# Graph network on one core: a longer buffer ring for the first edge pass, and the lookup's block differences made by TensorE and ScalarE

## The chip, the cores and the metric

One Trainium2 chip, one of its cores. The metric is the device time of one execution in microseconds (us), lower is better. The kernel before took 4364.09 us, the median of three runs (4363.95 to 4365.29).

## What is computed

A graph of 6250 nodes (padded to 6656, that is 52 blocks of 128) and 100000 edges sorted by destination (padded to 784 tiles of 128) goes through four layers. Each one normalizes x, takes the ReLU, runs a message pass over the edges and adds its result to x. Only the first layer, a graph attention, is touched:

```python
h = relu(layernorm(x))
hw = h @ W
a_s = hw @ att_src
a_d = hw @ att_dst
e = leaky_relu(a_s[src] + a_d[dst], 0.2)
m = segment_max(e, dst)
p = exp(e - m[dst])
out = segment_sum(hw[src] * (p / segment_sum(p, dst)[dst]), dst)
x = x + out + bias
```

In the kernel the sums over edges run on rows of h (128 floats of a node), and the product with W comes after them.

## The kernel before, in words

A tile is 128 edges, one per partition; a chunk is C = 8 tiles. For each tile GpSimd issues one indirect DMA that fetches the 128 source rows of h from `table[0]` in DRAM into a slot of a row buffer (a buffer holds one chunk, 4 KB per partition). These gathers are issued one after another by GpSimd, 784 for the layer. The ring has `RING0` = 16 buffers, four that live all through the kernel (`m.rows`) and twelve in `m.more`. `gather_straight` (L873) issues those gathers that need no free buffer, that is the first 16 * 8 = 128, spread over the phases ahead of the edge pass. A phase is a block: all engines begin it together and meet at its end. In order:

- `norm_phase` (L239) writes h to `table[0]` and its transpose to `m.hT` (a 128 x 6656 tile, 26 KB per partition).
- `setup_phase` (L107): SyncE loads five 392 KB index arrays, VectorE (after all five, `loaded` 80) splits the source index into its low 7 bits (`lo`, stored to DRAM) and its block number (`src_hi`, kept), and works out windows. GpSimd issues 14 gathers (`IN_SETUP`).
- `attention_tables_phase` (L407): TensorE spreads a_d over the nodes from `m.hT`; a_s is brought into columns. GpSimd issues 30 gathers (`IN_TABLES`).
- `lookup_phase` (L485) finds a_s[src] for every edge in 49 steps of 16 tiles. In a step SyncE loads the low bits broadcast to all partitions (`place`, 512 KB, ring of 4); VectorE turns them into a one-hot (`make`, L535, into `onehot`, bf16); TensorE multiplies it by a_s in three bf16 parts, 48 products of 52 columns (L560), which gives a candidate for each of the 52 blocks; GpSimd makes `away`, the block number counted from 0 to 51 less the edge's own (L521); VectorE keeps the candidate where `away` is zero (`pick`, L541) and sums over the blocks (`keep`, L547). VectorE's order is make of the next step, pick, keep. GpSimd's order is one `away`, one gather.
- `segment_max_phase` (L563): scans on VectorE and three trips through DRAM. GpSimd issues 20 gathers (`IN_MAXIMA`).
- `attention_edges` (L1102): GpSimd issues the last 15 of the first 128 gathers, then walks the ring (`gather_long_ring`, L954, which issues through L839): a gather waits until VectorE has freed its buffer (`rows_free`). For each of 98 chunks VectorE makes weights (`weigh`), TensorE clears a bank (L789) and adds up 8 tiles by a product with the rows (L1217) and one with ones (L1218), and VectorE adds the window into `acc` (L1193) and frees the buffer. VectorE's loop body holds 8 chunks, TensorE's as many as the ring.
- `attention_output` (L2086): SyncE sends three lines of sums to DRAM and brings them back in another layout, loads weights, then x in four slabs of 768 KB (or 832 KB). TensorE multiplies `acc` and `m.hT` by W, GpSimd adds the bias to x, ScalarE scales, and VectorE works out the shares of the softmax (L2167 to L2182) and adds both parts to x.

The later layers are not touched. What sets the order around the change is the program order of each engine's queue; there is no planner. Durations below belong to these lines.

Of the kernel before, what the change touches and what calls it, by code (L numbers as in the profile page):

```python
# [10 lines left out]
RING0 = 16  # L11
# [4 lines left out]
IN_SETUP, IN_TABLES, IN_MAXIMA = 14, 30, 20  # L16
# [90 lines left out]
def setup_phase(nc, k, m, early):  # L107

    T, NP, N = k.T, k.NP, k.N
    with ExitStack() as ctx:  # L110
# [7 lines left out]
        hi_i = sb("su_hi", [P, T], I32)  # L118
        span = sb("su_span", [P, 2, T], F32)
# [3 lines left out]
        lo_ready = sem("su_lo_ready")  # L123
        chain = sem("su_chain")
        stored = sem("su_stored")
        with nc.Block() as block:
            @block.sync
            def _(sp):
# [4 lines left out]
                sp.dma_start(hi_i[:], k.dram["src_el"]).then_inc(loaded, 16)  # L133
# [3 lines left out]
                sp.wait_ge(stored, 16)  # L137
                sp.wait_ge(loaded, 80)
# [7 lines left out]
            def _(v):  # L146
                ch = Chain(v, chain)
                v.wait_ge(loaded, 80)

                ch.step(v.tensor_scalar(lo_i[:], lo_i[:], P - 1, None, ALU.bitwise_and))  # L150
                v.tensor_copy(lo_b[:], lo_i[:]).then_inc(lo_ready, 1)
                ch.step(v.tensor_scalar(hi_i[:], hi_i[:], 7, None, ALU.logical_shift_right))
                ch.add(v.tensor_copy(m.src_hi[:], hi_i[:]))
# [331 lines left out]
def lookup_phase(nc, k, m, s_el, early):  # L485
# [5 lines left out]
    with ExitStack() as ctx:  # L491
# [4 lines left out]
        away, masked = [sb(f"away{b}", [P, L, NB], F32) for b in range(2)], [sb(f"masked{b}", [P, L, NB], F32) for b in range(2)]  # L496
        block_ps = [ctx.enter_context(nc.psum_tensor(f"lu_ps{b}", [P, L, PER], F32)) for b in range(2)]
        place_ready, place_free = [sem(f"place_ready{r}") for r in range(4)], sem("place_free")
        onehot_ready, block_ready, away_ready = sem("onehot_ready"), sem("block_ready"), sem("away_ready")
# [3 lines left out]
        steps = T // L  # L503
        with nc.Block() as block:
# [11 lines left out]
            def _(pool):  # L516
                pool.sem_inc(masked_ready, 2)

                for n in range(steps):
                    pool.wait_ge(masked_ready, n + 1)  # L520
                    pool.tensor_tensor(away[n % 2][:], m.iota_f[:, 0:NB].unsqueeze(1).to_broadcast([P, L, NB]),  # L521
                                       m.src_hi[:, n * L:(n + 1) * L].unsqueeze(2).to_broadcast([P, L, NB]),
                                       ALU.subtract).then_inc(away_ready, 1)
                    gather_straight(pool, k, m, early, k.table[0], IN_SETUP + IN_TABLES + n, 1)

            @block.vector
            def _(v):
                v.sem_inc(place_free, 4)
                v.sem_inc(block_ready, 2)
                v.sem_inc(picked, 2)  # L530

# [5 lines left out]
                def pick(at):  # L537
                    v.wait_ge(block_ready, at.n + 3)
                    v.wait_ge(away_ready, at.n + 1)
                    v.wait_ge(picked, at.n + 1)  # L540
                    v.scalar_tensor_tensor(masked[at.b][:], away[at.b][:], 0.0, block_ps[at.b][:, :, 0:NB], ALU.is_equal, ALU.mult).then_inc(masked_ready, 1)  # L541
# [11 lines left out]
            def _(pe):  # L553

                def product(at):
                    pe.wait_ge(onehot_ready, at.n + 1)
# [5 lines left out]
                    ins.then_inc(block_ready, 1)  # L562
                skewed(pe, steps, Item, [(0, product)])  # L563


def segment_max_phase(nc, k, m, s_el, early):
# [4 lines left out]
    with ExitStack() as ctx:  # L571
# [18 lines left out]
        with nc.Block() as block:  # L590
# [16 lines left out]
            def _(pool):  # L607
                gather_straight(pool, k, m, early, k.table[0], IN_SETUP + IN_TABLES + T // (2 * C), IN_MAXIMA)
# [254 lines left out]
def early_rows(nc, name, rows, begun):  # L863
# [4 lines left out]
    early.gathered = [[nc.alloc_semaphore(f"{name}gathered{r}_{q}") for q in range(2)] for r in range(len(rows))]  # L868
    early.idx_loaded, early.dst_loaded = nc.alloc_semaphore(name + "idx_loaded"), nc.alloc_semaphore(name + "dst_loaded")
    early.all = sum(early.gathered, []) + [early.idx_loaded, early.dst_loaded]  # L870
# [1976 lines left out]
```

## Time and profile before

| | before |
|---|---|
| median of three runs | 4364.09 us |
| the profiled execution's own time | 4362.5 us |
| its span, first to last instruction | 4360.7 us |
| TensorE, VectorE, ScalarE, GpSimd busy | 84%, 49%, 31%, 66% |
| TensorE clock, mean of the span | 0.667 of 2.4 GHz |
| setup block begins | 41.6 us |
| lookup block begins, ends | 105.6 us, about 269.7 us |
| first bank of the edge pass cleared, last sum added | 306.7 us, 1158.0 us |
| attention output, first transfer issued | 1161.3 us |

Times are measured from the first instruction. Matmul, weight load, VectorE, ScalarE and GpSimd instructions have a start and a duration; "idle before" is the time that an engine stood still ahead of an instruction, with what ended it. An indirect DMA on GpSimd counts as busy while GpSimd writes its descriptors; the rows themselves land later. In a table by stretches the column PEclk is the TensorE clock that was granted, as a share of 2.4 GHz (0.50 is 1.2 GHz).

### The profile page before, as it was taken

Reading aid. Unit: us, or ns where it says so; the run is one execution under the profiler, and the core shown is the slowest. Engines: PE = TensorE matmul, PEld = TensorE weight load, DVE = VectorE, ACT = ScalarE, POOL = GpSimd, SP = SyncE. Lnnn points to the kernel's source line nnn. Section 1 sums busy time; section 2 is a strip of 40 time slices with the busy share of each in tenths; the row PEclk is TensorE's granted clock in tenths of the full one; section 3 lists DMA queues with packets and bytes.
Section 4 is the critical chain, followed back from the end, with each engine's and each line's share of the span. In section 5 each row is a group of like instructions: output and inputs, shape, how many; then the busy total and the mean of one; then the engine's idle time right before and its main releaser. Section 6 shows DMA issues by size and latency. Waiting matters only on the chain. (4 is left out here: it accounts for less than half of the span.)

```text
span 4360.7 us, 76651 instructions
## 1 busy us (share of the span) xinstructions
PE 3646.0 (84%) x20596; PEld 3028.2 (69%) x20597; DVE 2136.9 (49%) x6551; ACT 1362.1 (31%) x1910; POOL 2881.8 (66%) x2980
## 2 busy tenths in 40 slices
PE   3649999777668999999996958888888865999997
PEld 1649999766637888888886846656555643777775
DVE  4874444333455555555554844444444446444442
ACT  2000000000041111111112847666666655444441
POOL 4877777777526777777751047777777764777772
PEclk7555555555575555555556978777777775999998
DMA  4532222222263333333322043333333333111112
GB/s 121 197 116 54 53 53 53 53 53 53 63 208 106 79 80 79 79 78 78 79 68 84 21 127 113 100 104 104 104 99 105 104 82 85 50 50 51 50 51 52
DMA packets 258518, 364.29 MB, mean 84 GB/s; under 512 B 53070, under 2 KB 179461, under 8 KB 258309
## 3 DMA queue, kind: packets, MB, share of 16 engines
q0 software_dynamic: 90624, 185.78, 16.5%
q1 hardware_dynamic: 167689, 176.37, 13.4%
q14 instruction: 148, 1.21, 0.1%
q8 instruction: 57, 0.93, 0.1%
HBM read 319.53 MB, written 42.41 MB: 83 GB/s over the span
## 5 line engine op out<-in xcount | busy, mean ns | idle before, releaser
L839 POOL DMA_INDIRECT m_rows<-table,e_idx x832 | 794.2, 955 | 255.8 <-issue 228.6
L839 POOL DMA_INDIRECT m_more<-table,e_idx x480 | 453.7, 945 | 145.6 <-issue 118.5
L1218 PE MATMUL e_agg<-e_weights,m_ones 128*128 128x32 f32 x1568 | 481.8, 401 | 0.0
L839 POOL DMA_INDIRECT m_hT<-table,e_idx x416 | 394.1, 947 | 125.7 <-issue 107.6
L1218 PEld LDWEIGHTS e_agg<-e_weights,m_ones 128*128 128x128 f32 x1568 | 428.5, 333 | 0.0
L839 POOL DMA_INDIRECT e_rows<-table,e_idx x352 | 342.0, 971 | 105.7 <-issue 103.9
L1217 PE MATMUL e_agg<-e_weights,m_more 128*128 128x16 f32 x1152 | 339.8, 375 | 78.3 <-issue 66.3
L1653 PE MATMUL e_z<-e_edge,e_w 128*128 128x512 f32 x392 | 262.8, 806 | 167.2 <-DVEq L1734 152.2
L805 POOL DMA_INDIRECT m_rows<-table,e_idx x320 | 307.9, 962 | 116.0 <-issue 82.3
L1217 PEld LDWEIGHTS e_agg<-e_weights,m_more 128*128 128x128 f32 x1152 | 311.5, 330 | 104.2 <-issue 104.2
L1542 PE MATMUL e_out<-e_counts,e_nodes 128*128 128x256 bf16 x2964 | 383.6, 280 | 0.0
L1882 PE MATMUL e_x<-e_key,e_rows_T 128*128 x1568 | 373.9, 420 | 2.5 <-DMA e_key<-key_dram 2.5
L1384 ACT ACTIVATE e_counts<-e_count 128x832 bf16<-128x832 f32 x304 | 262.4, 864 | 321.8 <-PE e_count L1535 321.2
L1882 PEld LDWEIGHTS e_x<-e_key,e_rows_T 128*128 128x128 f32 x1568 | 352.4, 330 | 9.3 <-issue 7.1
L1542 PEld LDWEIGHTS e_out<-e_counts,e_nodes 128*128 128x128 bf16 x2964 | 297.6, 100 | 79.5 <-issue 5.5
L1664 PEld LDWEIGHTS e_z<-e_w,e_filt 128*128 128x128 f32 x1568 | 257.4, 257 | 50.3 <-issue 50.3
L1664 PE MATMUL e_z<-e_w,e_filt 128*128 128x128 f32 x1568 | 282.4, 354 | 0.0
L1143 ACT ACTIVATE e_pl<-e_diff 128x8 f32<-128x8 f32 x98 | 20.6, 210 | 801.6 <-DVE e_diff L1177 801.6
L1653 PEld LDWEIGHTS e_z<-e_edge,e_w 128*128 128x128 f32 x392 | 88.0, 250 | 256.4 <-DVEq L1734 158.2
L1675 PE MATMUL e_agg<-e_onehot,e_message 128*128 128x16 f32 x1568 | 228.1, 289 | 12.5 <-DVE e_message L1746 12.3
L1843 ACT ACTIVATE e_p<-e_p 128x32 f32<-128x32 f32 x98 | 22.5, 229 | 684.8 <-DVEq L2011 684.8
L1675 PEld LDWEIGHTS e_agg<-e_onehot,e_message 128*128 128x128 f32 x1568 | 218.3, 223 | 20.6 <-issue 13.1
(315 smaller groups left out, 7057.3 us busy)
## 6 DMA issues: line engine op xcount, KB each, us to landing
e_edge<-edge_T SPq DMA_DIRECT2D x98, 512.0 KB
lu_place<-lo_dram SPq DMA_DIRECT2D x49, 512.0 KB, 3.8
e_key<-key_dram SPq DMA_DIRECT2D x98, 256.0 KB
m_rows<-table,e_idx POOLq DMA_INDIRECT x1152, 2.5
key_dram<-key_out SPq DMA_DIRECT2D x13, 1024.0 KB, 4.7
table<-m_rows SPq DMA_DIRECT2D x39, 256.0 KB, 2.6
e_rows<-table,e_idx POOLq DMA_INDIRECT x528, 2.6
m_more<-table,e_idx POOLq DMA_INDIRECT x480, 2.5
```

Source lines behind the costliest of these rows:

```text
L805: pool.indirect_dma_start(rows[:, t, :], None, table, bass.IndirectOffsetOnAxis(ap=idx[:, t:t + 1], axis=0)).then_inc(landed[q], 16)
L839: pool.indirect_dma_start(rows[:, t, :], None, table, bass.IndirectOffsetOnAxis(ap=idx[:, t:t + 1], axis=0)).then_inc(landed[t * len(lande ...
L1143: act.activation(pl[b][:, :, 0], diff[:], ACT.Exp).then_inc(p_ready, 1)
L1217: pe.matmul(to[:, 0, cols], s.rows[at.r][:, t, :], both[:, t, 0, :], start=False, stop=False)
L1218: ins = pe.matmul(to[:, 1:3, cols], m.ones[:], both[:, t, :, :], start=False, stop=(t == C - 1))
L1384: act.activation(counts[at.b][:, :, t * W_NARROW:(t + 1) * W_NARROW].rearrange("p (h n) w -> p h n w", h=2), count_ps[t % 2][:, :, 0:PART] ...
L1542: ins = pe.matmul(out_ps[b][:, 0:L * W_NARROW], nodes[:, part, block_no, :], counts[b][:, block_no, :], start=(i == 0), stop=(i == 3 * NB ...
L1653: ins = pe.matmul(z1[:, cols], w1[:], edge[at.b][:, cols], start=True, stop=True)
L1664: ins = pe.matmul(z2[at.b][:, cols], filt1[at.b][:, cols], w2[:], start=False, stop=(t % G4 == G4 - 1))
L1675: ins = pe.matmul(agg[at.b][:, ds(rel[t], W)], message[at.b][:, t * P:(t + 1) * P], s.onehot[at.b][:, t * W:(t + 1) * W], start=False, sto ...
L1843: act.activation(p[:], p[:], ACT.Exp).then_inc(p_ready, 1)
L1882: ins = pe.matmul(to[:, q * HEADS * W:(q + 1) * HEADS * W], rows_T[:, t, :], key[at.b][:, :, ds(rel[t], W)], start=True, stop=True)
```

## The change

`RING0` goes from 16 to 24. The eight new buffers: two more in `m.more` (which has 14 then), and six laid over `m.hT`, which is dead between the attention tables and the attention output. ScalarE's DMA queue stores those columns of `m.hT` (6144 of 6656, 3.1 MB in four transfers) to DRAM during the lookup, and loads them back at the start of the attention output; the first gather into them waits for the stores. In the lookup `away` is no longer made by GpSimd. The block number of each edge is stored to DRAM in setup and loaded in a layout of 16 rows; with a row of ones, two bf16 products of 17 rows and 416 columns give the differences in PSUM, and ScalarE copies them to SBUF (128x832 per step), into the place of the last two ring buffers. GpSimd only gathers there, 9 gathers in 4 steps, 110 in all where there were 49. The gathers ahead of the edge pass are 14 + 30 + 110 + 26 = 180 where there were 113; in the pass 12 follow without a wait, then 592 through the ring where there were 656. One of the five loads of setup is gone and one store (196 KB) is new. A row buffer has one semaphore, not two.

```diff
-RING0 = 16
+RING0 = 24
+OVER_HT = 6
-IN_SETUP, IN_TABLES, IN_MAXIMA = 14, 30, 20
+IN_SETUP, IN_TABLES, IN_MAXIMA = 14, 30, 26
+def lookup_gathers(step):
+    return step * 9 // 4
...
 # setup_phase
-                sp.dma_start(hi_i[:], k.dram["src_el"]).then_inc(loaded, 16)
+                sp.wait_ge(hi_ready, 1)
+                sp.dma_start(k.dram["hi_dram"].rearrange("(p t) -> p t", p=P), hi_b[:]).then_inc(stored, 16)
-                v.wait_ge(loaded, 80)
+                v.wait_ge(loaded, 64)
+                ch.step(v.tensor_scalar(hi_i[:], lo_i[:], 7, None, ALU.logical_shift_right))
+                v.tensor_copy(hi_b[:], hi_i[:]).then_inc(hi_ready, 1)
...
 # lookup_phase
-        away, masked = [sb(f"away{b}", [P, L, NB], F32) for b in range(2)], ...
+        last_rows = (RING0 - RING - OVER_HT - 2) * C * P
+        away = [m.more[:, last_rows + b * L * NB:last_rows + (b + 1) * L * NB].rearrange("p (l n) -> p l n", n=NB) for b in range(2)]
+        hi_T, away_of = sb("hi_T", [L + 1, T // L, P], BF16), sb("away_of", [L + 1, L, NB], BF16)
+                sp.dma_start(hi_T[1:L + 1, :, :], k.dram["hi_dram"].rearrange("(n t p) -> t n p", t=L, p=P)).then_inc(hi_loaded, 16)
...
                 for n in range(steps):
                     pool.wait_ge(masked_ready, n + 1)
-                    pool.tensor_tensor(away[n % 2][:], ..., ALU.subtract).then_inc(away_ready, 1)
-                    gather_straight(pool, k, m, early, k.table[0], IN_SETUP + IN_TABLES + n, 1)
+                    gather_straight(pool, k, m, early, k.table[0], IN_SETUP + IN_TABLES + lookup_gathers(n),
+                                    lookup_gathers(n + 1) - lookup_gathers(n))
+            @block.scalar
+            def _(act):
+                for n in range(4):
+                    part = hi_T[0:1, parts[n]:parts[n + 1], :].rearrange("p n d -> p (n d)")
+                    act.activation(part, m.ones[0:1, 0:1].to_broadcast([1, part.shape[1]]), ACT.Copy).then_inc(ones_ready, 1)
+                over = OVER_HT * C * P // 4
+                def take(at):
+                    act.wait_ge(numbers_ready, at.n + 1)
+                    act.wait_ge(masked_ready, at.n + 1)
+                    act.activation(away[at.b], away_ps[at.b][:, :, 0:NB], ACT.Copy).then_inc(away_ready, 1)
+                for n in range(4):
+                    act.dma_start(k.dram["hT_dram"][:, n * over:(n + 1) * over], m.hT[:, n * over:(n + 1) * over]
+                                  ).then_inc(early.hT_kept, 16)
+                skewed(act, steps, Item, [(0, take)])
...
                 def product(at):
+                    pe.wait_ge(away_ready, at.n + 1)
+                    for half in range(2):
+                        tiles = slice(half * L // 2, (half + 1) * L // 2)
+                        ins = pe.matmul(away_ps[at.b][:, tiles, 0:NB], hi_T[:, ds(at.n, 1), :].rearrange("k n p -> k (n p)"), away_of[:, tiles, :],
+                                        start=True, stop=True)
+                    ins.then_inc(numbers_ready, 1)
                     pe.wait_ge(onehot_ready, at.n + 1)
                     pe.wait_ge(masked_ready, at.n + 1)
...
+                pe.wait_ge(hi_loaded, 16)
+                pe.wait_ge(away_of_ready, 2)
+                pe.wait_ge(ones_ready, 4)
...
 # gather_straight
+    over_hT = (RING0 - OVER_HT - 2) * C
     for n in range(first, min(first + count, len(early.rows) * C)):
+        if n == over_hT:
+            pool.wait_ge(early.hT_kept, 64)
...
 # attention_output
+                    if g * GN < 4 * over:
+                        pe.wait_ge(hT_loaded[g * GN // over], 16)
...
             def _(act):
+                for n in range(4):
+                    cols = slice(n * over, (n + 1) * over)
+                    act.dma_start(m.hT[:, cols], k.dram["hT_dram"][:, cols]).then_inc(hT_loaded[n], 16)
...
 # build: the ring in order
+            early = early_rows(nc, "g0_", [rows[:] for rows in m.rows] + [rows_of(m.more, n) for n in range(own - 2)] +
+                               [rows_of(m.hT, n) for n in range(OVER_HT)] + [rows_of(m.more, n) for n in (own - 2, own - 1)],
```

## Rows read from the trace of the kernel before

**Rows 1.** Stretches: us, busy PE, PEld, DVE, ACT, POOL, then PEclk, DMA share, GB/s:
```profile
106.00:270.00 164.00, 110.67 (x2352) 104.06 (x2352) 146.61 (x147) 0.00 (x0) 137.32 (x98) 0.50 0.56 184
326.00:785.00 459.00, 442.28 (x1975) 418.47 (x1974) 212.33 (x1137) 16.44 (x63) 347.13 (x369) 0.50 0.20 53
785.00:1158.00 373.00, 276.57 (x1224) 259.41 (x1224) 129.45 (x690) 10.13 (x38) 274.38 (x293) 0.50 0.20 52
```
**Rows 2.** Timeline of the edge pass, the cleared banks (start us, duration, instruction):
```profile
324.64 0.50 PE L789 MATMUL e_agg<-m_zeros 1*128 1x384 bf16 x1
...
777.99 0.50 PE L789 MATMUL e_agg<-m_zeros 1*128 1x384 bf16 x1
```
**Rows 3.** Timeline of the edge pass, GpSimd's first and last ring gathers, and its end:
```profile
326.60 0.97 POOL L839 DMA_INDIRECT m_rows<-table,e_idx  x1 [2.61 <-DVEq L1196]
...
1146.10 0.95 POOL L839 DMA_INDIRECT m_rows<-table,e_idx  x1 [0.30 <-issue]
1157.21 0.80 DVE L1193 TENSOR_TENSOR m_acc<-m_acc,e_agg 128x128 f32 x3 [10.32 <-PE e_agg L1218]
```
**Rows 4.** DMA issues of setup, with the us from issue to landing:
```profile
su_lo<-src_el_t SPq DMA_DIRECT2D x1, 392.0 KB, 6.6
su_hi<-src_el SPq DMA_DIRECT2D x1, 392.0 KB, 8.3
```
**Rows 5.** Timeline of one step in the middle of the lookup:
```profile
258.51 1.24 POOL L878 DMA_INDIRECT m_more<-table,m_src_idx  x1
258.84 1.01 DVE L541 SCALAR_TENSOR_TENSOR lu_masked<-lu_away,lu_ps 128x832 f32<-128x832 f32 x1
258.98 2.26 PE L560 MATMUL lu_ps<-m_as_part,lu_onehot 128*128 128x52 bf16 x48 [0.89 <-DVE lu_onehot L535]
259.93 1.58 POOL L521 TENSOR_TENSOR lu_away<-m_iota_f,m_src_hi 128x832 f32<-128x832 f32 x1 [0.17 <-DVE lu_masked L541]
260.92 1.13 DVE L535 TENSOR_SCALAR lu_onehot<-lu_place,m_part_f 128x2048 bf16<-128x2048 bf16 x1
261.98 1.01 DVE L541 SCALAR_TENSOR_TENSOR lu_masked<-lu_away,lu_ps 128x832 f32<-128x832 f32 x1
```
**Rows 6.** Timeline of the lookup, its start and its end:
```profile
114.40 0.75 DVE L535 TENSOR_SCALAR lu_onehot<-lu_place,m_part_f 128x2048 bf16<-128x2048 bf16 x1 [10.87 <-DMA lu_place<-lo_dram]
117.51 1.02 DVE L541 SCALAR_TENSOR_TENSOR lu_masked<-lu_away,lu_ps 128x832 f32<-128x832 f32 x1 [1.05 <-PE lu_ps L560]
...
268.61 1.02 DVE L547 TENSOR_REDUCE m_s_el<-lu_masked 128x16 f32<-128x832 f32 x1
```
**Rows 7.** Timeline of the segment maxima, and ScalarE's first instruction behind them:
```profile
273.59 1.79 DVE L647 TENSOR_TENSOR_SCAN sg_run<-sg_bars,m_s_el 128x784 f32<-128x784 f32 x1
274.08 2.05 POOL L878 DMA_INDIRECT m_more<-table,m_src_idx  x1 [0.30 <-issue]
...
298.90 0.94 POOL L878 DMA_INDIRECT m_more<-table,m_src_idx  x1 [0.30 <-issue]
304.64 5.75 ACT L482 ACTIVATE m_acc<-m_ones 128x6656 f32<-128x6656 f32 x1 [1.82 <-PEq L89]
```
**Rows 8.** A stretch of the attention tables, columns as in rows 1:
```profile
78.00:85.00 7.00, 7.00 (x15) 1.28 (x14) 2.06 (x4) 2.39 (x4) 5.34 (x6) 1.00 0.22 57
```
**Rows 9.** Timeline of the next phase, where table stores run beside 3.4 MB of x:
```profile
1235.57 1.65 ACT L335 ACTIVATE m_rows<-m_more,n_shift,n_rstd 128x128 f32<-128x128 f32 x4 [6.59 <-DMA table<-m_rows]
```
**Rows 10.** Timeline of the attention output, from the lines' load to the shares:
```profile
1165.90 0.34 SPq L2117 DMA_DIRECT2D o_lines<-line_dram  x1
1170.89 0.38 DVE L2167 COPY o_cols<-o_lines_ps 128x208 f32<-128x208 f32 x1 [12.88 <-PE o_lines_ps L2143]
1180.97 0.65 DVE L2182 TENSOR_TENSOR o_share<-o_e,o_whole 128x104 f32<-128x104 f32 x1
```
**Rows 11.** Timeline of setup, a gather and the VectorE instruction that ran beside it:
```profile
51.25 1.16 POOL L878 DMA_INDIRECT m_rows<-table,m_src_idx  x1 [0.30 <-issue]
51.73 0.57 DVE L150 TENSOR_SCALAR su_lo<-su_lo 128x784 int32<-128x784 int32 x1 [10.68 <-DMA su_hi<-src_el]
```

More of the change, by code:

```diff
@@ L503, in lookup_phase @@
         steps = T // L
+        parts = [steps * n // 4 for n in range(5)]
         with nc.Block() as block:
@@ L607, in _ @@
             def _(pool):
-                gather_straight(pool, k, m, early, k.table[0], IN_SETUP + IN_TABLES + T // (2 * C), IN_MAXIMA)
+                gather_straight(pool, k, m, early, k.table[0], IN_SETUP + IN_TABLES + lookup_gathers(T // (2 * C)), IN_MAXIMA)
             @block.tensor
@@ L867, in early_rows @@
     early.rows, early.begun = rows, begun
-    early.gathered = [[nc.alloc_semaphore(f"{name}gathered{r}_{q}") for q in range(2)] for r in range(len(rows))]
+    early.gathered = [[nc.alloc_semaphore(f"{name}gathered{r}")] for r in range(len(rows))]
     early.idx_loaded, early.dst_loaded = nc.alloc_semaphore(name + "idx_loaded"), nc.alloc_semaphore(name + "dst_loaded")
-    early.all = sum(early.gathered, []) + [early.idx_loaded, early.dst_loaded]
+    early.hT_kept = nc.alloc_semaphore(name + "hT_kept")
+    early.all = sum(early.gathered, []) + [early.idx_loaded, early.dst_loaded, early.hT_kept]
     return early
 def gather_straight(pool, k, m, early, table, first, count):
+    over_hT = (RING0 - OVER_HT - 2) * C
     for n in range(first, min(first + count, len(early.rows) * C)):
+        if n == over_hT:
+            pool.wait_ge(early.hT_kept, 64)
         pool.indirect_dma_start(early.rows[n // C][:, n % C, :], None, table,
-                                bass.IndirectOffsetOnAxis(ap=m.src_idx[:, n:n + 1], axis=0)).then_inc(early.gathered[n // C][n % C // (C // 2)], 16)
+                                bass.IndirectOffsetOnAxis(ap=m.src_idx[:, n:n + 1], axis=0)).then_inc(early.gathered[n // C][0], 16)
 def first_turn(pool, k, m, early, table):
@@ L2106, in attention_output @@
         own = [m.rows[b][:, G4:2 * G4, :] for b in range(2)]
+        over = OVER_HT * C * P // 4
+        hT_loaded = [a.sem(f"hT_loaded{n}") for n in range(4)]
         x_loaded = [a.sem(f"x_loaded{n}") for n in range(len(slabs(k)))]
@@ L2735, in build @@
             ad = sbuf(layer, "ad", [P, k.NP])
-            m.more = sbuf(layer, "more", [P, (RING0 - RING) * C * P])
-            rows_of = lambda n: m.more[:, n * C * P:(n + 1) * C * P].rearrange("p (t d) -> p t d", d=P)
-            early = early_rows(nc, "g0_", [rows[:] for rows in m.rows] + [rows_of(n) for n in range(RING0 - RING)],
-                               IN_SETUP + IN_TABLES + k.T // (2 * C) + IN_MAXIMA)
+            own = RING0 - RING - OVER_HT
+            m.more = sbuf(layer, "more", [P, own * C * P])
+            rows_of = lambda t, n: t[:, n * C * P:(n + 1) * C * P].rearrange("p (t d) -> p t d", d=P)
+            early = early_rows(nc, "g0_", [rows[:] for rows in m.rows] + [rows_of(m.more, n) for n in range(own - 2)] +
+                               [rows_of(m.hT, n) for n in range(OVER_HT)] + [rows_of(m.more, n) for n in (own - 2, own - 1)],
+                               IN_SETUP + IN_TABLES + lookup_gathers(k.T // (2 * C)) + IN_MAXIMA)
             with ExitStack() as first:
@@ L2744, in build @@
                     norm_phase(nc, k, m, "n0_", k.table[0], x_from=k.dram["x_in"], early=early, measured=False)
[L2745 removed]
+                m.as_part = sbuf(first, "as_part", [P, 3, k.NB], BF16)
                 with ExitStack() as su:
```

35 lines of the change are left out of this document (19 added, 16 removed).

## The prediction, made before the changed kernel was run

> **What bounds the first layer now.** Four views, in this order. The table by stretches [rows 1] says which engine is full when: in the lookup VectorE (146.6 of 164 us), in the first 459 us of the edge pass TensorE (442 us), in the last 373 us TensorE no longer (277 us), while GpSimd keeps one pace throughout. So the pass has two halves: TensorE first eats the head start, then waits for gathers. The cleared banks [rows 2] give TensorE's own pace: 59 chunks from 324.64 to 777.99 us, 7.68 us each. GpSimd's first and last ring gather [rows 3] give the other pace: 655 steps from 326.60 to 1146.10 us, 1.251 us each, 10.0 us a chunk. The pass ends 11.9 us after the last gather's start (1158.01 less 1146.10) [rows 3]. GpSimd sets that end, and a gather taken out of the ring is worth 1.251 us, as long as TensorE would be done earlier.
>
> **The edge pass.** 592 ring gathers instead of 656: 64 x 1.251 = **80.1 us less**. Is TensorE done by then? Its bank of chunk 97 could be cleared at 324.64 + 96 x 7.68 = 1062.3, the pass be over 8.4 us later, at about 1071; by the gathers it is over at 1158.0 - 80.1 = 1077.9. So GpSimd still ends it, by 7 us, and only the last four chunks wait. The pass is now nearly balanced: any further head start would give 7 us at most. The first ring gather waits, as now, for the first buffer to be freed; the 12 gathers ahead of it take 15 us and fit before that. VectorE's body stays at 8 chunks. TensorE's body of 24 chunks has no row; I take nothing for it (TensorE's pace at its body of 16 holds all its costs), and 2 us either way.
>
> **Setup.** VectorE starts when all loads have landed. The fourth load lands 6.6 us after its issue, the fifth, issued 0.47 us later, 8.3 us [rows 4], so without the fifth the start is up to 2.2 us earlier; half of that if bandwidth alone counts. I take **-1.6 us** (-2.2 to -1.0). The instructions on VectorE are the same number; the new 196 KB store is covered by 12 us of VectorE work behind it.
>
> **The lookup, VectorE's side.** A step takes 3.14 us (pick 258.84 to pick 261.98), and VectorE is never idle in it [rows 5]. `make` takes 1.13 us there, beside `away` on GpSimd, but 0.75 us when GpSimd is still [rows 6, 5]. With `away` gone from GpSimd I price a step at 3.14 - 0.38 = 2.76 us. From the first `make` to the end (114.40 to 269.63) are 155.2 us, 49.4 steps: **-18.8 us**. Below that it cannot go, since pick, keep and make remain. The 128x832 copy on ScalarE hides: ScalarE has no other work there, and 5.75 us for 6656 columns [rows 7] is 0.7 us of 2.76.
>
> **TensorE's side.** 48 products of 52 columns take 2.26 us at half clock (2496 columns, 0.905 ns each) [rows 5]. The two new ones have 832 columns: 0.75 us by that row, 1.08 us by the cleared bank's 0.50 us for 384 columns [rows 2], which holds the tail. So at half clock TensorE needs 3.06 us a step (up to 3.39) and becomes the bound; at full clock it needs about half and hides. Which is it? At half clock TensorE would have no pause; in the attention tables a stretch without a pause has the clock at 1.00 [rows 8], but the edge pass, 96% busy, stays at 0.50 [rows 1]. The lookup's stream of short loads and products without pause is between them. I take the higher clock for enough of the steps that VectorE sets 2.76 us. The Trainium skill, page "TensorE: Matmul & The Clock Gate", Part 1, says that being busy lifts the throttle; by that rule the sum is as here, though the edge pass disagrees with it as it stands.
>
> **GpSimd's side.** 110 gathers instead of 49, each 0.95 + 0.30 us if nothing holds it. Its row beside `make` is 1.24 us: from 258.51, where `make` ended at 258.92 [rows 5], and in the maxima a scan from 273.59 to 275.38 held the gather of 274.08 to 2.05 us [rows 7]; in both it ended 0.75 to 0.83 us after VectorE let go. So one that comes up during `make` waits for its end. Stepping by 1.25 us from the end of a `make`, the third falls into the next (2.5 us against 2.0 to 2.76), so two get through per step where 2.25 are asked. After 46 steps some 14 are left, 17.5 us, of which 4.5 run beside the last picks and keeps: the block ends **13 us** after VectorE (4 if nothing holds them). So a part of the head start is bought on the path. SyncE's extra issue ahead of the `place` loads: **+0.4**. The 3.1 MB stores and 61 more gathers beside `place` loads: the engines' share is 0.56 now [rows 1]; I take **+1** (0 to 5). The row of ones on ScalarE (four times 1568 columns, 6 us by [rows 7]) ends before the first `make`.
>
> **Segment maxima.** GpSimd's last gather ends at 299.84, the block at 304.64 - 1.82 = 302.82 [rows 7]. Six more take 7.5 us and end at 307.3: **+4.5**. GpSimd sets that end now.
>
> **Attention output.** The load of 3.1 MB starts when the block does, beside the small round trip of the lines (issued 1165.90, used 1170.89) and ahead of x. Table stores beside 3.4 MB of x waited 6.6 us longer in the next phase [rows 9], twice in a row; nothing is the lower bound, since products of group 0 need only the first quarter. Against it, GpSimd's bias additions, which stretch VectorE's small steps between 1170.89 and 1180.97 [rows 10], would start later too. I take **+4** (0 to 16).
>
> **The sum.** -1.6 + 0.4 - 18.8 + 13 + 1 + 4.5 - 80.1 + 4 = -77.6 us against the profiled execution's 4362.5, so 4284.9; the median stands 1.6 us higher, so **4287 us**. The later layers have the same instructions.
>
> **Rivals.** (a) **TensorE stays at half clock in the lookup** and bounds it at 3.06 us: 49.4 x (3.06 - 3.14) = -4.0 instead of -18.8, so 4301; at 3.39 us a step 4318. For it: 0.50 in every stretch of [rows 1]. (b) **Gathers hold up `make`**, as `away` did, and it stays at 1.13 us: a step of 3.14, 4305. Against it: a tensor_scalar of setup took 0.57 us beside a gather that had begun before it [rows 11], and so did its neighbours. The Trainium skill, "SBUF — State Buffer", section "Who interferes with whom", says the shared port pair is locked for a whole instruction by whoever comes first, which speaks against this change; by it (b) would come, but that row disagrees in this direction, while [rows 7] agree in the other. (c) **Nothing holds the gathers**: 9 us off, 4278. (d) **Slower than before: VectorE holds every gather of the lookup** as the scan did, 2.05 + 0.30 us [rows 7]. From 117.4, 106 gathers end at 366.5 instead of 269.6: +96.9 + 4.5 - 80.1 + 4 = +25, 4389. It decides from 2.1 us a gather on. Against it: pick reads one operand from PSUM and let a gather through at 1.24 [rows 5]. (e) **The head start is not there**, because what is gathered early is paid in full: it would need the lookup to end 72 us later, the mechanism of (d) at its turning point, 4364.
>
> **How the numbers follow.** Forecast 0.45; (a) 0.28; (b) 0.09; (c) 0.11; (d) and (e) 0.03 and 0.01; 0.03 for a cost that no row shows. The low end is (c) with a free attention output and no late `place`: 4273, and 5 us for TensorE's loop and for setup: 4268. The high end is (a) at its upper price, which (b) and a full 16 us of reload on the forecast also stay under: 4318. About 0.2% (9 us) is what a measurement of this kernel can tell from no change. Faster by more 0.95, within it 0.01 (case e), slower 0.04 (case d and a third of the unnamed costs).
>
> **What would show it.** Right: the first ring gather still some 20 us after the pass begins, then 592 of them at 1.25 us without a wait; TensorE's pace 7.68 us until the last few chunks; in the lookup `make` at 0.75 us, picks 2.76 us apart, the clock above 0.5 in part of it, GpSimd last by about 13 us. Wrong: picks 3.06 us apart at 0.50 (a); `make` at 1.13 (b); gathers of 2 us in the lookup (d); a chunk pace over 7.75 us, by which TensorE ends the pass; VectorE's first step of the attention output over 10 us later than now.

## The result, and the profile after

The changed kernel took 4380.82 us (median of six runs, 4375.30 to 4383.06); the kernel before took 4364.38 beside it. The ratio is 1.0037, with an interval of 1.0025 to 1.0050: **slower by about 16 us**, where 4287 was forecast, in a range of 4268 to 4318. The execution that was profiled, and that the tables below read, was the fastest of the six; it took 13 us more than the one of the kernel before.

| | before | after |
|---|---|---|
| the profiled execution's own time | 4362.5 us | 4375.3 us |
| its span | 4360.7 us | 4371.8 us |
| TensorE, VectorE, ScalarE, GpSimd busy | 84%, 49%, 31%, 66% | 83%, 49%, 32%, 64% |
| lookup block begins | 105.6 us | 105.2 us |
| the block of the edge pass begins | 304.6 us | 319.6 us |
| first ring gather | 326.6 us | 403.2 us |
| attention output, first transfer issued | 1161.3 us | 1162.7 us |

The table by stretches of the kernel after, columns as in [rows 1], which it answers:

```profile
106.00:270.00 164.00, 119.08 (x2450) 89.65 (x2450) 129.63 (x149) 47.24 (x53) 115.51 (x110) 0.69 0.71 228
326.00:785.00 459.00, 438.32 (x1955) 414.46 (x1955) 212.47 (x1139) 15.75 (x63) 296.83 (x314) 0.50 0.18 46
785.00:1158.00 373.00, 288.30 (x1279) 271.07 (x1280) 133.91 (x721) 9.25 (x39) 275.56 (x291) 0.50 0.21 52
```

The second row is the one to look at. GpSimd ran 314 instructions in 459 us, nearly all of them gathers, where it had run 369. It was forecast to start as now and keep its pace of 1.25 us; it did not start. The timeline of the edge pass after, with the first bank, the end of the gathers that ask for nothing, the first and the last ring gather and the end [answering rows 2 and 3]:

```profile
321.64 0.49 PE L832 MATMUL e_agg<-m_zeros 1*128 1x384 bf16 x1 [11.09 <-issue]
...
334.08 0.95 POOL L925 DMA_INDIRECT m_more<-table,m_src_idx  x1 [0.30 <-issue]
335.04 0.37 POOL L1047 COPY e_idx<-m_src_idx 128x192 int32<-128x192 int32 x1
403.24 0.98 POOL L882 DMA_INDIRECT m_rows<-table,e_idx  x1 [67.83 <-DVEq L1243]
...
1147.11 0.95 POOL L882 DMA_INDIRECT m_rows<-table,e_idx  x1 [0.30 <-issue]
1158.56 0.80 DVE L1240 TENSOR_TENSOR m_acc<-m_acc,e_agg 128x128 f32 x3 [10.61 <-PE e_agg L1265]
```

**GpSimd stood still for 67.8 us**, waiting for VectorE to free a buffer (the releaser is VectorE's queue at the line that frees one), while all 24 buffers were filled or being filled. In [rows 3] the same wait was 2.61 us. So the pass, from the block's start to the first output transfer, went from 856.7 us (304.64 to 1161.32) to 843.1 (319.55 to 1162.67): the 64 gathers fewer were saved, and 61.7 us more passed ahead of the first ring gather (403.24 - 319.55 = 83.7, against 326.60 - 304.64 = 22.0).

The waits of GpSimd in the whole trace after say that it was one wait and not many (us in total, times, longest):

```profile
POOL m_rows L882 <- DVEq L1243: 67.8, 1, 67.8
```

TensorE waits between 320 and 1160 us for rows that have not landed, 81 us in 31 waits (the first, third and fourth line), all of them behind 785 us:

```profile
PE e_agg L1264 <- DMA m_more<-table,e_idx: 42.1, 16, 3.4
PE e_agg L1264 <- DVEq L1233: 25.3, 9, 10.4
PE e_agg L1264 <- DMA m_hT<-table,e_idx: 23.2, 9, 3.7
PE e_agg L1264 <- DMA m_rows<-table,e_idx: 15.8, 6, 3.9
```

That is nearly what the kernel before has behind 785 us, 95.5 us in 37 waits, for most of which its profile names no releaser:

```profile
PE e_agg L1217 <- issue: 90.4, 35, 3.7
```

So TensorE eats the head start and then waits for GpSimd as it did before; with the wait put right (experiment 1) 17.1 us of this are left.

The whole ledger in us, block by block (the block of the maxima begins with SyncE's first transfer, at 270.33 us before and 278.99 after):

| | before | after | difference | forecast |
|---|---|---|---|---|
| setup | 22.9 | 22.0 | -0.9 | -1.6 |
| lookup: block start to first `make` | 8.9 | 15.6 | +6.7 | +1.4 |
| lookup: first `make` to VectorE's end | 155.2 | 137.9 | -17.3 | -18.8 |
| lookup: VectorE's end to the next block | 0.7 | 20.4 | +19.7 | +13 |
| segment maxima | 34.3 | 40.6 | +6.3 | +4.5 |
| edge pass | 856.7 | 843.1 | -13.6 | -80.1 |
| attention output, to its first store of x | 60.0 | 69.6 | +9.6 | +4 |

With +0.6 us ahead of setup and +0.2 behind the layer they make the 11 us by which the spans differ. One term is off by 66.5 us; the six others are off by 0.7 to 6.7 us each, and all of them are dearer than forecast.

The cause can be read in the code, in the function that walks the ring (L1053), which the diff does not touch:

```python
pool.wait_ge(s.rows_free[r % shared], turn * (ring // shared) + r // shared)
```

There are 8 semaphores (`shared`), each begins at 1, and VectorE adds 1 to one of them for each chunk it has used. Buffer r of turn t is to be filled again when chunk 24(t - 1) + r is done, and that chunk's semaphore then stands at (t - 1) x 3 + r // 8 + 2. The line asks for t x 3 + r // 8, which is **one more: the chunk 8 further on, 16 behind the gather's own instead of 24**. With 16 buffers (t - 1) x 2 + 2 and t x 2 are the same number. So a ring of 24 runs like one of 16: its first ring gather waits for chunk 8, not for chunk 0. In time: 19.9 us from the first bank to the first freed buffer (measured below), and 8 x 7.68 [rows 2] = 61.4 us for 8 chunks more, is 81.3; measured are 403.24 - 321.64 = 81.6.

### The profile page after: what moved, and what is told of

Read it like the earlier page. It is cut to its first block and busy times, and to the rows that moved or that the text cites. A ratio compares the mean times of both kernels' runs of the same rounds, so it can differ in the third digit from the quotient of the medians.

```text
span 4371.8 us, 76778 instructions
## 1 busy us (share of the span) xinstructions
PE 3645.6 (83%) x20694; PEld 3014.4 (69%) x20695; DVE 2123.1 (49%) x6553; ACT 1407.7 (32%) x1961; POOL 2809.4 (64%) x2929
## 5 line engine op out<-in xcount | busy, mean ns | idle before, releaser
L882 POOL DMA_INDIRECT m_rows<-table,e_idx x768 | 739.1, 962 | 301.6 <-issue 217.6
L882 POOL DMA_INDIRECT m_hT<-table,e_idx x560 | 535.1, 956 | 169.6 <-issue 145.4
L882 POOL DMA_INDIRECT m_more<-table,e_idx x336 | 320.6, 954 | 102.0 <-issue 80.4
L848 POOL DMA_INDIRECT m_rows<-table,e_idx x320 | 306.2, 957 | 113.7 <-issue 84.7
L1264 PE MATMUL e_agg<-e_weights,m_more 128*128 128x16 f32 x896 | 264.4, 376 | 48.4 <-DMA m_more<-table,e_idx 42.1
L1264 PEld LDWEIGHTS e_agg<-e_weights,m_more 128*128 128x128 f32 x896 | 242.4, 331 | 68.1 <-issue 68.1
```

The source lines that it names most:

```text
L848: pool.indirect_dma_start(rows[:, t, :], None, table, bass.IndirectOffsetOnAxis(ap=idx[:, t:t + 1], axis=0)).then_inc(landed[q], 16)
L882: pool.indirect_dma_start(rows[:, t, :], None, table, bass.IndirectOffsetOnAxis(ap=idx[:, t:t + 1], axis=0)).then_inc(landed[t * len(lande ...
L1264: pe.matmul(to[:, 0, cols], s.rows[at.r][:, t, :], both[:, t, 0, :], start=False, stop=False)
```

## The experiments

The theory: the wait value alone turned the sign (A). The rivals: the pass is bound by TensorE or by something else that the 24 buffers bring, and the lookup or the stores cost what was gained (B). The kernel before stood beside them at 4360.53 us (experiments 1, 2, 3 and 5), 4361.61 us (the first two runs of 4, then 6 and 7) and 4369.15 us (the repetitions in 4 and 8).

**1. The wait put right, and nothing else.**

```diff
-pool.wait_ge(s.rows_free[r % shared], turn * (ring // shared) + r // shared)
+pool.wait_ge(s.rows_free[r % shared], (turn - 1) * (ring // shared) + r // shared + 2)
```

> The changed kernel with one number of the ring wait changed: a gather into a buffer waits until the chunk 24 earlier has been freed. As it was written for 24 buffers it waited for the chunk 16 earlier. Theory A (the wait made the ring 16 long): the first ring gather starts some 20 us after the pass begins, where it stood still for 67.8 us before; 592 gathers at 1.255 us then end the pass about 775 us after its first bank, where it was 837.7: 62 us less, 4319 us. Theory B (the head start is lost elsewhere, in TensorE's pace or in the gathers' landing): the stall moves to another engine and the time stays within 10 us of the changed kernel's 4380.8.

Measured: 4313.7 us, ratio 0.9890 (0.9874 to 0.9907). The difference to the kernel after is 0.0147 of 4362 us, 64 us, by one number in one line. Its edge pass (timeline: first bank, first and last ring gather, end):

```profile
320.95 0.49 PE L832 MATMUL e_agg<-m_zeros 1*128 1x384 bf16 x1 [11.37 <-issue]
...
340.81 0.98 POOL L882 DMA_INDIRECT m_rows<-table,e_idx  x1 [6.08 <-DVEq L1243]
...
1085.46 0.95 POOL L882 DMA_INDIRECT m_rows<-table,e_idx  x1 [0.30 <-issue]
1096.59 0.80 DVE L1240 TENSOR_TENSOR m_acc<-m_acc,e_agg 128x128 f32 x3 [10.34 <-PE e_agg L1265]
```

The first ring gather comes 19.9 us after the first bank, as forecast, and the pass takes 781.9 us (318.86 to 1100.79): 74.8 less than before, for 80.1 forecast. The missing 5.3 us are the pitch of the gathers: (1085.46 - 340.81) / 591 = 1.260 us, where [rows 3] give 1.251; 592 x 0.009 = 5.3. TensorE waits for rows only from 1030 us on. Its waits, in the stretch up to there and in the one behind it:

```profile
PE e_agg L1264 <- DVEq L1233: 30.1, 12, 10.4
PE e_agg L832 <- issue: 12.6, 3, 11.4
...
PE e_agg L1264 <- DMA m_rows<-table,e_idx: 6.5, 2, 3.7
PE e_agg L1264 <- DMA m_more<-table,e_idx: 5.4, 2, 2.7
PE e_agg L1264 <- DMA m_hT<-table,e_idx: 5.2, 2, 2.6
```

The first two lines are of 320 to 1030 us, the last three of 1030 to 1101. Only in the second stretch does a row come late: six waits, 17.1 us, where four were forecast. The two engines are nearly balanced, and GpSimd ends the pass.

**2. The same fault put into the kernel before.** If A is right, a wait value one too high costs the kernel before the same 60 us, without a new lookup, new buffers or stores.

```diff
-pool.wait_ge(s.rows_free[r % shared], turn * (ring // shared) + r // shared)
+pool.wait_ge(s.rows_free[r % shared], turn * (ring // shared) + r // shared + 1)
```

> The kernel before with one added to the value that a ring gather waits for, so that its ring of 16 works like one of 8. Theory A (a wait one too high costs eight chunks of TensorE's pace at the start, and nothing later): the first ring gather starts some 61 us later, the 656 gathers follow at 1.251 us, 4425 us. Theory B (gathers are so far behind that the wait does not matter): no change, 4364.

Measured: 4421.05 us (one run), 60.5 above the kernel before. GpSimd's timeline has the same picture as after:

```profile
390.63 0.97 POOL L839 DMA_INDIRECT m_rows<-table,e_idx  x1 [64.86 <-DVEq L1196]
```

The cost of the wait is shown from both sides: 64 us back when it is taken out of one kernel, 60.5 lost when it is put into the other.

**3. Sixteen buffers with the new lookup.** `RING0` is 16, nothing lies over `m.hT`, nothing of it is stored or loaded, one gather a step in the lookup and 20 in the maxima: what the lookup gives by itself. The line of the ring wait is that of experiment 1, which gives the same number as the old one for 16 buffers.

```diff
-RING0 = 24
-OVER_HT = 6
-IN_SETUP, IN_TABLES, IN_MAXIMA = 14, 30, 26
-    return step * 9 // 4
+RING0 = 16
+OVER_HT = 0
+IN_SETUP, IN_TABLES, IN_MAXIMA = 14, 30, 20
+    return step
```

> The change's lookup alone: 16 buffers, nothing laid over the turned node rows and nothing of them stored or loaded back, 49 gathers in the lookup and 20 in the maxima as before. The pass is then as before (656 ring gathers). Theory A: the lookup's VectorE part takes 138 us instead of 155 and no stores delay its first one-hot, so the pass begins 16 to 18 us earlier and the time is 4347. Theory B (the new lookup costs as much as it gives, by TensorE's clock or by ScalarE): within 5 us of before, 4364.

Measured: 4347.95 us, ratio 0.9976 (0.9966 to 0.9985). The first `make` starts at 113.77 us, the last keep at 250.79, SyncE's first transfer of the next block is at 252.72, 17.6 us earlier than before (270.33). So **the new lookup is worth 13 us by itself by the medians (10 by the ratio), and the ring gives 34 us more** when its wait is right (37 by the ratios): not 80. The traces of experiments 3 and 1 say where the rest goes. The pass is 80.6 us shorter, but the transfers of `m.hT` cost some 16 us (first `make` at 120.32 instead of 113.77, attention output 69.7 us instead of 60.4), and the gathers moved ahead cost 19 us more in the rest of the lookup block and 7 in the maxima.

**4. How the gathers of the lookup are paid.** With the right wait, one gather a step (49 in all), then two (98), beside the 110 of experiment 1:

```diff
-    return step * 9 // 4
+    return step          # 49
+    return step * 2      # 98
```

> Right wait, and 49 gathers in the lookup instead of 110, all else as in the first kernel; 73 gathers then come in the pass ahead of the ring. Theory A (an early gather of the lookup is bought for a part of its price): the lookup ends 19 us earlier, the first ring gather comes 72 us later after the pass begins, 53 us more than the first kernel, 4366; the closing drain of GpSimd takes 5 us, not 10. Theory B (the lookup's price eats the head start): within 15 us of 4314.

> Right wait, and 98 gathers in the lookup, two a step. Theory A: GpSimd keeps up with VectorE, its last gather comes 10 us earlier, the pass's first ring gather 15 us later after the pass begins, so 2 to 5 us more than the first kernel, 4317. If the closing drain grows with the gathers issued since the last one it takes 8 to 9 us here; if it depends on GpSimd being late it takes 4 to 5, and the time falls by 1 us instead.

With 49: 4366.95 us (one run), as expected; 61 gathers less in the lookup put 61 more ahead of the ring, and the first ring gather is at 392.62 us. All of the head start has to be made before the pass; 24 buffers without it are worth nothing, and stand 19 us behind the 16 buffers of experiment 3, which have no transfers of `m.hT`. With 98: 4305.82 us (one run), where 4317 were expected. **The expectation had the wrong sign**: 12 gathers fewer made the kernel faster. (Its second branch, that the end of the block takes 8 to 9 us if it grows with the gathers issued, came: 8.93.) The timeline at the change from the lookup to the maxima shows why; the idle time of the first gather of the maxima was ended by GpSimd's own queue, that is, by the end of the block. With 49 gathers in the lookup:

```profile
258.87 1.21 POOL L925 DMA_INDIRECT m_more<-table,m_src_idx  x1 [5.60 <-POOLq L519]
```

With 98, from the last gather of the lookup on:

```profile
253.99 1.02 POOL L925 DMA_INDIRECT m_hT<-table,m_src_idx  x1 [0.30 <-issue]
263.95 1.21 POOL L925 DMA_INDIRECT m_hT<-table,m_src_idx  x1 [8.93 <-POOLq L519]
```

The kernel after, with 110, from VectorE's last keep on:

```profile
257.62 1.02 DVE L580 TENSOR_REDUCE m_s_el<-lu_masked 128x16 f32<-128x832 f32 x1
268.34 0.95 POOL L925 DMA_INDIRECT m_hT<-table,m_src_idx  x1 [0.30 <-issue]
279.21 1.21 POOL L925 DMA_INDIRECT m_hT<-table,m_src_idx  x1 [9.91 <-POOLq L519]
```

At two a step GpSimd ends with VectorE (253.99 us). At nine in four steps it is 10.6 us behind it (269.29 against 258.64): with the right wait too, the next block begins 14.7 us later with 110 than with 98 (278.43 against 263.73), and in the pass the 12 gathers would cost 12 x 1.260 = 15.1 us. So they gained nothing; and 6.1 us of the 15.1 would have been free in the pass, since GpSimd waited so long for the first buffer (340.81 us, above). By this sum 98 are 14.7 - 15.1 + 6.1 = 5.7 us better than 110. Both traces with 98 agree: the attention output begins at 1095.52 and 1095.83 us, against 1100.79 with 110.

> The right wait with two gathers per lookup step, timed once more for the same reason. If the one earlier run of 4305.8 us was typical: 4306 us, within 3 us, against 4313.7 with 110 gathers in the lookup. If it was a low draw: 4310 to 4314 us.

Measured: 4311.61 us beside 4369.15 for the kernel before, ratio 0.9867 (0.9851 to 0.9884), where 110 gathers had 0.9890 (0.9874 to 0.9907). The plain time falls into the range named for a low draw, but the kernel before was 8 us slower on this occasion too, and the ratio is that of the one run (0.9872). The two intervals overlap, so the gain rests on the 5 us that the traces show, not on these ratios.

**5. The stores and the reload moved out of the way.** ScalarE's stores of `m.hT` are issued at the lookup's start, ahead of the first `place` loads; the timeline of the kernel after:

```profile
105.33 2.04 ACTq L551 DMA_DIRECT2D hT_dram<-m_hT  x3
...
107.39 1.47 ACTq L551 DMA_DIRECT2D hT_dram<-m_hT  x1
...
108.14 6.27 SPq L528 DMA_DIRECT2D lu_place<-lo_dram  x4
...
120.76 0.75 DVE L568 TENSOR_SCALAR lu_onehot<-lu_place,m_part_f 128x2048 bf16<-128x2048 bf16 x1 [14.04 <-DMA lu_place<-lo_dram]
```

Here they wait until the first pick, and the reload of `m.hT` waits until the lines have landed:

```diff
-                for n in range(4):
-                    act.dma_start(k.dram["hT_dram"]...)
+                    if isinstance(at.n, int) and at.n == 1:
+                        act.wait_ge(masked_ready, 3)
+                        for n in range(4):
+                            act.dma_start(k.dram["hT_dram"]...)
 # attention_output
+                act.wait_ge(lines_loaded, 64)
```

> The first of these kernels (right wait), with the stores of the turned rows issued after the lookup's first pick instead of at its start, and their reload in the attention output issued once the round trip of the lines has landed. Theory A (the 3.1 MB transfers delay small ones ahead of them): the first one-hot starts 6 us earlier, the shares of the attention output are ready up to 8 us earlier, 4305 to 4309 us. Theory B (the transfers are hidden by other work): within 4 us of the first kernel.

Measured: 4306.77 us, ratio 0.9878 (0.9862 to 0.9895), 5 us below experiment 1 by the ratio. The first `make` starts 6.6 us earlier than in experiment 1 (120.32) and the attention output is 3.0 us shorter (66.7 against 69.7 us). The block after the lookup, though, starts only 2.9 us earlier (275.52 against 278.43), and VectorE's last keep too (254.58 against 257.50): `make` now waits for `place` some steps later, beside the stores. In all it waits for `place` 11.1 us in 4 waits, against 14.5 in 2. So more than half of what the stores cost was only moved. Its first `make` in the timeline, and one of the later waits:

```profile
113.72 0.75 DVE L570 TENSOR_SCALAR lu_onehot<-lu_place,m_part_f 128x2048 bf16<-128x2048 bf16 x1 [7.03 <-DMA lu_place<-lo_dram]
...
134.43 0.75 DVE L570 TENSOR_SCALAR lu_onehot<-lu_place,m_part_f 128x2048 bf16<-128x2048 bf16 x1 [2.80 <-DMA lu_place<-lo_dram]
```

The intervals of the ratios of experiments 1, 5, 6 and 7 overlap from one to the next. What orders them is the end of the layer in their traces, the first store of x of the attention output: 1170.46, 1164.58, 1156.09 and 1148.54 us.

**6. The lines ahead of the products.** In experiment 5 TensorE's first group of products waits for the first quarter of `m.hT` while the three lines lie ready behind it in its queue. So the group moves behind them:

```diff
-                products(0)
                 ...
-                for g in range(1, NG):
+                for g in range(NG):
```

> Right wait, late stores, late reload, and in the attention output TensorE turns the lines before its first group of products, so that the softmax shares no longer wait for the first quarter of the reloaded rows. Theory A: the stretch from the block's first transfer to the next block falls from 66.7 us to 60 to 62 us (60.0 before the change), the time by 5 to 7 us against the late reload alone, 4300 us. Theory B (x, which shares the transfer engines with the reload, sets the pace): no change, 4306.

Measured: 4299.4 us, ratio 0.9859 (0.9843 to 0.9876). The attention output is 56.9 us long (1099.21 to 1156.09), less than the 60.0 before. VectorE's copy of the lines and its shares in the timeline of the kernel after:

```profile
1180.90 0.38 DVE L2221 COPY o_cols<-o_lines_ps 128x208 f32<-128x208 f32 x1 [21.54 <-PE o_lines_ps L2194]
...
1192.12 0.65 DVE L2236 TENSOR_TENSOR o_share<-o_e,o_whole 128x104 f32<-128x104 f32 x1
```

The same two here, with one of the small steps between them and GpSimd's first bias additions:

```profile
1106.56 0.38 DVE L2223 COPY o_cols<-o_lines_ps 128x208 f32<-128x208 f32 x1 [10.86 <-PE o_lines_ps L2195]
...
1107.32 0.21 DVE L2227 TENSOR_TENSOR o_e<-o_e,o_cols 128x52 f32<-128x52 f32 x1
...
1109.43 3.72 POOL L227 TENSOR_TENSOR m_more<-m_more,o_bias 128x512 f32<-128x512 f32 x3 [24.92 <-DMA m_more<-x_in]
1110.12 0.69 DVE L2238 TENSOR_TENSOR o_share<-o_e,o_whole 128x104 f32<-128x104 f32 x1
```

From the copy to the shares 3.6 us pass instead of 11.2: VectorE's small steps are now nearly through when GpSimd's bias additions begin. In the kernel before they ran beside them too (10.1 us, [rows 10]). The same small step took 1.34 us there, just behind the start of the bias additions, and 0.21 here:

```profile
1171.63 16.90 POOL L219 TENSOR_TENSOR m_more<-m_more,o_bias 128x512 f32<-128x512 f32 x13 [24.59 <-DMA m_more<-x_in]
1171.64 1.34 DVE L2171 TENSOR_TENSOR o_e<-o_e,o_cols 128x52 f32<-128x52 f32 x1
```

**7. Fewer gathers in the maxima.**

```diff
-IN_SETUP, IN_TABLES, IN_MAXIMA = 14, 30, 26
+IN_SETUP, IN_TABLES, IN_MAXIMA = 14, 30, 22
```

> The same with 22 gathers in the segment maxima instead of 26. GpSimd stands still for 6.1 us ahead of its first ring gather in the pass, room for four gathers. Theory A (a gather taken early is worth nothing while that pause is there, and costs 1.25 us where GpSimd ends the block): 4 to 5 us less than the run beside it, 4296. Theory B (every early gather is worth its 1.25 us): same time, as cost and worth cancel.

Measured: **4294.6 us, ratio 0.9845 (0.9829 to 0.9862), the lowest of all, 67 us below the kernel before.** Its first ring gather waits 1.08 us for the first buffer:

```profile
332.66 0.98 POOL L884 DMA_INDIRECT m_rows<-table,e_idx  x1 [1.08 <-DVEq L1245]
```

**8. Both: 22 in the maxima and two a step.**

> The best version so far (right wait, stores and reload later, lines first, 22 gathers in the segment maxima), with two gathers per lookup step, 98 in all, instead of 110. Theory A: the last 12 gathers cost about 14.7 us at the end of the lookup block and 12 x 1.257 = 15.1 us in the edge pass, where GpSimd now has no pause left, so GpSimd ends the pass at the same time: 4295 us, within 4 us, with the lookup block 14 to 15 us shorter and 28 gathers without a wait ahead of the first ring gather, still near 333 us. Theory B: the 12 gathers are dearer in the lookup than in the pass for another reason than the pause (with the 26 gathers in the maxima, one run of two per step came 8 us below the version of 110): 4287 to 4290 us.

> The right wait with two gathers per lookup step, timed this time (one run gave 4305.8 us). If the one run was typical: 4306 us, within 3 us, against 4313.7 with 110 gathers in the lookup. If it was a low draw: 4310 to 4314 us.

These two do not answer the question: on that occasion the kernel before took 5633.76 us itself, and these two 5644.76 (ratio 1.0012, 0.9978 to 1.0047) and 5666.62 (1.0048, 1.0011 to 1.0084). In the trace of the first, TensorE stood still for 401 us in 62 waits ahead of its products with the rows (330 to 1400 us), and for 261 us of them the profile names nothing on this core that it waited for. What slowed all three is not known; it does mean that in such surroundings nothing of the 67 us is gained. They were made again:

> The best version so far with two gathers per lookup step (98 in all) once more, since the kernel before itself took 5634 us beside the first try. Theory A (the last 12 gathers cost in the lookup what they are worth in the pass, because GpSimd has no pause left): 4295 us, within 4 us. Theory B (they are dearer in the lookup for another reason): 4287 to 4290 us.

Measured: 4303.54 us beside 4369.15 for the kernel before, ratio 0.9849 (0.9833 to 0.9866), the same as experiment 7's 0.9845; the first store of x comes at 1152.59 us, 4 us later than in experiment 7, where theory B has it 5 to 8 us earlier. Theory A holds: once GpSimd no longer pauses before the ring, the last 12 gathers cost as much in the lookup as in the pass. (Its edge pass begins at 297.49 us instead of 310.71, and its first ring gather is at 334.30 instead of 332.66.)

## Why the prediction was wrong

**The step that failed** is "The first ring gather waits, as now, for the first buffer to be freed; the 12 gathers ahead of it take 15 us and fit before that." The gathers ahead of it did fit; the wait was not for the first buffer but for chunk 8, and 61.7 us more passed before the first ring gather. The number waited for is worked out from the ring's size in a function outside the diff, and was not worked out for 24. Case (e), "The head start is not there", came nearest, with 4364 us and a chance of 0.01, but it was tied to slow gathers in the lookup. The head start was there, all 192 gathers of it; it was the use of it that was held back. With the wait right, the kernel takes 4313.7 us, inside the range and 27 us above the forecast.

Those 27 us, term by term, from the ledger and experiment 1:

- **The edge pass, -80.1: with the right wait -74.8.** The mechanism was right, TensorE's pace held until 1030 us, GpSimd ended the pass. Each gather was 0.009 us dearer.
- **The lookup on VectorE, -18.8: -17.3.** `make` took 0.74 to 0.76 us in 48 of 49 steps, as the row without `away` had said, and picks are 2.75 to 2.77 us apart for 2.76 forecast in most steps. A step in the timeline of the kernel after [answering rows 5]:

```profile
149.41 1.01 DVE L574 SCALAR_TENSOR_TENSOR lu_masked<-m_more,lu_ps 128x832 f32<-128x832 f32 x1
149.55 1.40 PE L599 MATMUL lu_ps<-m_as_part,lu_onehot 128*128 128x52 bf16 x48
149.92 0.95 POOL L925 DMA_INDIRECT m_more<-table,m_src_idx  x1 [0.30 <-issue]
150.56 1.02 DVE L580 TENSOR_REDUCE m_s_el<-lu_masked 128x832 f32 x1
150.88 0.52 PE L592 MATMUL lu_away<-lu_away_of,lu_hi_T 17*128 17x416 bf16 x2
151.17 1.19 POOL L925 DMA_INDIRECT m_more<-table,m_src_idx  x1 [0.30 <-issue]
151.50 0.74 DVE L568 TENSOR_SCALAR lu_onehot<-lu_place,m_part_f 128x2048 bf16<-128x2048 bf16 x1
152.16 1.01 DVE L574 SCALAR_TENSOR_TENSOR lu_masked<-m_more,lu_ps 128x832 f32<-128x832 f32 x1
```

- **Rival (a), half clock, did not come.** The 48 products take 1.40 us here, against 2.26 at half clock [rows 5], and the granted clock of the stretch is 0.69, that is, 2.4 GHz in part of it and 1.2 in the rest: the 48 products take 1.40 us in 18 steps and 2.26 in 20. In the kernel after, TensorE was busy for 5.00 of 5.00 us from 125 to 130 us, at a granted 0.50, and in the ten us behind that the mean is 0.78. The two new products take 0.52 us at the higher clock. (The prediction's 3.06 and 3.39 us a step at half clock are 0.05 us more than the terms it gives for them.) The Trainium skill, page "TensorE: Matmul & The Clock Gate", Part 1, says that being busy lifts the throttle; the lookup agrees (its clock went from 0.50 to 0.69 with more work in it), and the edge pass, busy for 438 of 459 us at 0.50, still disagrees.
- **Rival (b) did not come.** The gather of 151.17 us runs over `make`, and `make` takes 0.74 us; one `make` of the 49 took 0.97. The Trainium skill, page "SBUF — State Buffer", section "Who interferes with whom", has the one that comes first lock the pair of ports for its whole instruction; here GpSimd came first and did not hold VectorE up, as in [rows 11], while the gather was held (1.19 us instead of 0.95). In the other direction the prediction's rule holds: a gather that comes up during `make` waits for its end. In 25 steps of the kernel after a gather began inside a `make`, and each ended 0.81 to 0.83 us behind it (252.86 against 252.03 here), as in [rows 5]:

```profile
251.29 0.74 DVE L568 TENSOR_SCALAR lu_onehot<-lu_place,m_part_f 128x2048 bf16<-128x2048 bf16 x1
251.67 1.19 POOL L925 DMA_INDIRECT m_hT<-table,m_src_idx  x1 [0.30 <-issue]
```

- **GpSimd's tail, +13: +19.7.** Two gathers get through per step, as forecast (149.92 and 151.17, then 152.67 and 153.93), and the last ends 10.6 us after VectorE. What was left out is the end of the block on GpSimd: 9.91 us idle before the next gather. With 49 gathers it is 4.93 us before and 5.60 in experiment 4, and there part of it ran beside VectorE's last steps.
- **SyncE and `place`, +1.4: +6.7.** The range of 0 to 5 for the stores was too narrow, since they came ahead of the loads, not beside them. Without the stores (experiment 3) the first `make` comes 8.4 us after the block's start, where it was 8.9 before. Issued later they let it begin 6.6 us earlier, of which 2.9 us were left at VectorE's end (experiment 5).
- **The segment maxima, +4.5: +6.3**, GpSimd last, as forecast. The forecast put the block's end at the end of the last gather; here too the queue took longer, 3.9 us (315.68 to 319.55).
- **The attention output, +4: +9.6.** The lines were used 10.9 us after their load was issued (1170.05 to 1180.90), where 5.0 us passed before [rows 10]: the load itself had been issued 7.4 us after the block's start instead of 4.6 (4.6 again in experiment 5, where the 3.1 MB come behind the lines), and the bias additions then fell on the small steps just as before. It was not forecast that the hiding place, the products of group 0, would itself hold the lines up in TensorE's queue; experiments 5 and 6 show that, 66.7 us with it and 56.9 without.
- **Setup, -1.6: -0.9.**

The differences add up to 5.3 + 1.5 + 6.7 + 5.3 + 1.8 + 5.6 + 0.7 = 26.9 us. Each cost of making the head start was taken at a middle value, and each came out dearer. The kernel that was forecast lies 63 us above the high end of the range, and the one wait carries it there.

The chance of 0.04 for slower was too small for a change whose gain hangs on a number that the diff does not show. The profile of before could not show it either, since with 16 buffers the number is right; the code could.

## What to carry to other kernels

When the depth of a ring changes, work out for its first refill which use each wait stands for, in every function that the ring goes through and above all in those that the diff leaves alone: a wait one too high changes nothing in what is computed and makes the extra buffers useless. Work moved ahead of a stage is free only where its engine would stand still; count what it adds at the end of the block it is moved into, the closing wait of its queue too, and stop where the next piece costs as much there as where it came from. Stores that make room for a prefetch belong behind the loads on which the block begins, but look whether they only hold up later loads then: here 2.9 of 6.6 us stayed.

## What was not expected of the hardware

- **The end of a block on GpSimd takes longer the more gathers have been issued in it.** In the kernel after, the idle time before the next block's first gather was 3.08 us with 14 gathers (setup), 4.48 with 26 (the maxima) and 9.91 with 110 (the lookup); it was 8.93 with 98, and at most 4.93 and 5.60 with 49, where the block waited for VectorE as well. What GpSimd does in that time no run separates.
- **The granted clock of the lookup rose to 0.69** with 98 small products more and shorter steps. The 48 products took 1.40 us at one level and 2.26 at the other.
- **What a gather loses beside VectorE hangs on when it begins.** Inside a `make` it ended 0.81 to 0.83 us behind it, beside the scan 0.75 us behind it (2.05 us in all, [rows 7]); one that began 0.33 us ahead of a `make` ended 0.12 us behind it (1.19 us). Beside pick and keep it took 0.95. So two go through in 2.75 us.
- **GpSimd's additions made VectorE's small steps some six times as long**: 1.34 and 1.19 us beside them, 0.21 without (128x52, experiment 6).
- **The pitch of ring gathers is 1.260 us in experiment 1, against 1.251 before.** It does not come from the longer ring: with 16 buffers and the new lookup (experiment 3) it is 1.259 too, and 1.251 in experiment 2. Which part of the new code does it is open.
